# An eight-batch gated scan with a routed expert: statistics, normalising and turning of the next x moved to other engines

## The reference, cut to what matters

```
n = layernorm(x)                                   # over the 256 features
logits = n @ gate_W                                # 4 mixers; the best 2, softmax over them
for m in 0..3:
  g, v, d = n @ Wg[m] + bg[m], n @ Wv[m] + bv[m], n @ Wd[m] + bd[m]
  a = 0.001 + 0.998 * sigmoid(d)
  h[m] = scan over the tokens: h_t = a_t * h_(t-1) + sigmoid(g_t) * tanh(v_t)
t = x + layernorm(sum over m of weight[m] * h[m])
z = layernorm(t) * ln_g + ln_b
e = argmax(softmax(batchnorm(mean of z over the tokens) @ Wr + br)); gate = its probability
y = (relu(z @ W_down[e] + b_down[e]) @ W_up[e] + b_up[e]) * gate
out = t + layernorm(y)
```

## Time and profile before

| | us |
|---|---|
| median of 3 runs | 713.51 |
| profiled execution, whole time | 712.26 |
| its span on the core | 710.5 |
| TensorE busy | 646.5 (91%) |
| VectorE busy | 597.7 (84%) |
| ScalarE busy | 459.0 (65%) |
| GpSimd busy | 123.3 (17%) |

### The profile page before, as it was taken

One profiled execution on the slowest core, in us unless ns is written; L12 is line 12 of the kernel. 1 busy time (PEld: TensorE's weight loads), 2 busy tenths in 40 slices (PEclk: granted clock), 3 DMA queues, 4 the chain that ended last, 5 costly groups with the idle time before them and its releaser, 6 DMA issues. The chain is left out here.

```text
span 710.5 us, 11434 instructions
## 1 busy us (share of the span) xinstructions
PE 646.5 (91%) x3609; PEld 351.4 (49%) x3609; DVE 597.7 (84%) x1320; ACT 459.0 (65%) x813; POOL 123.3 (17%) x182
## 2 busy tenths in 40 slices
PE   3999989999999999999999999999999999898163
PEld 2445545555545555555545555555544554454151
DVE  6584999889997889889997889889997889788946
ACT  2748648875787548775787548775787545866113
POOL 2001032004310052004410052003410032001201
PEclk9999999999999999999999999999999999999555
DMA  8700130020202030020202030020200010000003
GB/s 225 193 1 0 60 119 1 1 71 27 94 1 71 3 123 1 1 71 22 99 1 70 3 123 1 1 71 21 100 1 11 3 60 0 12 1 0 0 12 118
DMA packets 34595, 31.86 MB, mean 45 GB/s; under 512 B 5814, under 2 KB 34522, under 8 KB 34522
## 3 DMA queue, kind: packets, MB, share of 16 engines
q1 hardware_dynamic: 34524, 31.00, 13.9%
HBM read 21.03 MB, written 8.39 MB: 41 GB/s over the span
## 5 line engine op out<-in xcount | busy, mean ns | idle before, releaser
L1192 PE MATMUL ps_main<-xh,w_hi 128*128 128x512 f16 x768 | 292.3, 381 | 2.4 <-ACT xh L512 1.5
L1192 PE MATMUL ps_main<-xh,w_lo 128*128 128x512 f16 x768 | 292.3, 381 | 0.0
L1192 PE MATMUL ps_main<-xl,w_hi 128*128 128x512 f16 x768 | 292.1, 380 | 0.0
L800 DVE TENSOR_TENSOR_SCAN hid<-decay_s,value_s 128x1024 f32<-128x1024 f32 (+1 forms) x64 | 144.6, 2260 | 6.7 <-DVE value_s L820 1.4
L533 ACT ACTIVATE decay_s<-ps_main,vecs 128x512 f32<-128x512 f32 x128 | 88.5, 692 | 61.8 <-PE ps_main L1192 57.4
L533 ACT ACTIVATE value_s<-ps_main,vecs 128x512 f32<-128x512 f32 x128 | 88.8, 694 | 60.4 <-PE ps_main L1192 60.4
L533 ACT ACTIVATE gate_s<-ps_main,vecs 128x512 f32<-128x512 f32 x128 | 88.1, 688 | 54.8 <-PE ps_main L1192 52.8
L1192 PEld LDWEIGHTS ps_main<-xl,w_hi 128*128 128x128 f16 x768 | 75.4, 98 | 91.4 <-issue 1.4
L1192 PEld LDWEIGHTS ps_main<-xh,w_hi 128*128 128x128 f16 x768 | 75.4, 98 | 87.1 <-ACT xh L512 1.8
L1192 PEld LDWEIGHTS ps_main<-xh,w_lo 128*128 128x128 f16 x768 | 75.3, 98 | 83.1 <-issue 0.8
L813 DVE SCALAR_TENSOR_TENSOR mixed<-ps_aux,comb,mixed 128x256 f32<-128x256 f32 x192 | 77.2, 474 | 16.8 <-PE ps_aux L1202 15.0
(11 more groups left out here) (167 smaller groups left out, 636.5 us busy)
## 6 DMA issues: line engine op xcount, KB each, us to landing
x_in<-in_L_attn_x SPq DMA_DIRECT2D x16, 512.0 KB, 4.4
resid<-in_L_attn_x SPq DMA_DIRECT2D x7, 1024.0 KB, 5.2
out<-resid SPq DMA_DIRECT2D x7, 1024.0 KB, 4.5
expert<-experts SPq DMA_DIRECT2D x8, 192.5 KB, 2.2
w_stage<-in_L_attn_Wg SPq DMA_DIRECT2D x4, 256.0 KB, 3.8
w_stage<-in_L_attn_Wd SPq DMA_DIRECT2D x4, 256.0 KB, 5.4
w_stage<-in_L_attn_Wv SPq DMA_DIRECT2D x4, 256.0 KB, 5.5
u_split<-in_L_ffn_W_down SPq DMA_DIRECT2D x4, 256.0 KB
```

The costliest lines, as they stand in the source:

```text
L800: dve.tensor_tensor_scan(states(pc), staged(decay_s, pc, pc.c), staged(value_s, pc, pc.c), start, ALU.mult, ALU.add).then_inc(scanned, 1)
L1192: ins = pe.matmul(ps_main[:, i % BANKS], w[:, 3 * m + kind, k, half * P:(half + 1) * P], v[:, bt.par, k, chunk(c)], start=(n == 0), stop=( ...
```

## The change

- **Statistics of the next x.** VectorE's 8 bn_stats go. ScalarE reads x twice: `sum_x` (8 copies with an accumulated row sum, ahead of banks 1 to 4) and `square_x` (8 squares of x minus mean with an accumulated row sum, ahead of banks 6 to 9). GpSimd makes the mean after the first and scale and shift after the second (`fold_x`, 5 small operations in place of 11).
- **Two copies of the normalised x.** `normalise_x` on ScalarE now writes fp16 directly (`x_tok`, high part, tokens on partitions) and stands ahead of banks 12 to 15. GpSimd makes the same rows in fp32 (`plain_x`, 8 tensor_scalar of 128x256, new), behind `fold_x` and ahead of `power`. VectorE subtracts them in two operations of 128x1024 (`split_x`), where `low_x` stood.
- **Turning by DMA.** `turn_x`, `high_x` and `low_x` are gone for all batches but the first. SyncE issues two transposing DMAs, one for the high and one for the low part, 128x2048 fp16 each, ahead of the expert's load. Products and gates wait for `x_fed`. The next load of x waits for `x_plain` in place of `x_normed`.
- **Positions.** With pv: normalise_t, turn_u, high_u, shares, router, route, down, high_h, turn_h of mixer 1, up and the start of the mix each stand one bank later.
- **Router mean of the last batch.** `sum_rows`, `shift_sum` and `rows_in` are gone; `route_in` sums the accumulators of the four `high_u` copies, as in the other batches, so it stands behind both turn_u.

The diff, cut (the first part is SyncE, then GpSimd, ScalarE, VectorE, TensorE):

```diff
@@ -359,9 +366,19 @@
                 sp.dma_start(resid[:, b.par], x_t[bass.ds(b.n, 1)].rearrange("a p t d -> p (a t) d")
                              ).then_inc(resid_loaded, 16)
 
+            def turn_x(b):
+
+                for half, split in ((0, xh_split), (1, xl_split)):
+                    sp.wait_ge(split, b.n)
+                    if half == 0:
+                        sp.wait_ge(main_filled, EVAC * b.n - EVAC + 1)
+                    sp.sem_inc(turn_begun, 1)
+                    sp.dma_start_transpose(x_feat[:, b.par, half].rearrange("p t k j -> p (t k) j"),
+                                           x_tok[:, half].rearrange("p t d -> p (t d)")).then_inc(x_fed, 16)
...
             def run(j, r, full=True):
                 b, back = Batch(2 * j + r, r % 2, False), Batch(2 * j + r - 1, 1 - r % 2, False)
+                turn_x(Batch(2 * j + r + 1, 1 - r % 2, False))
                 load_expert(back)
...
-                pool.tensor_tensor(mom[:, 1], even[:, :, 2], odd[:, :, 2], ALU.add)
-                link(pool.tensor_tensor(mom[:, 4], mom[:, 3], fold_const["square"][:], ALU.mult))
-                link(pool.tensor_tensor(mom[:, 3], mom[:, 4], mom[:, 1], ALU.add))
-                pool.tensor_tensor(mom[:, 0], even[:, :, 1], odd[:, :, 1], ALU.add)
-                link(pool.tensor_tensor(root_in["x"][:], mom[:, 3], fold_const["eps"][:], ALU.add))
+                pool.wait_ge(x_summed, nx.n)
+                link(pool.tensor_tensor(x_mean[:], x_row_sum[:], fold_const["mean"][:], ALU.mult))
+                pool.sem_inc(x_centred, 1)
+                pool.wait_ge(x_squared, nx.n)
+                link(pool.tensor_tensor(root_in["x"][:], x_row_square[:], fold_const["eps"][:], ALU.add))
                 link(pool.tensor_tensor(root_in["x"][:], root_in["x"][:], neg_half[:], ALU.pow))
-                pool.tensor_tensor(mul_by["x"][:], root_in["x"][:], fold_const["by"][:], ALU.mult)
-                link(pool.tensor_tensor(mom[:, 1], mom[:, 0], neg_half[:], ALU.mult))
-                pool.tensor_tensor(shift["x"][:], mom[:, 1], mul_by["x"][:], ALU.mult).then_inc(x_scaled, C)
+                pool.tensor_tensor(mul_by["x"][:], root_in["x"][:], fold_const["by"][:], ALU.mult).then_inc(x_factor, 1)
+                pool.wait_ge(x_factor, C + nx.n)
+                pool.tensor_tensor(shift["x"][:], x_mean[:], mul_by["x"][:], ALU.mult).then_inc(x_scaled, C)
+
+            def plain_x(nx):
+
+                pool.wait_ge(x_scaled, done(nx))
+                pool.sem_inc(plain_begun, 1)
+                for t in range(T):
+                    ins = pool.tensor_scalar(normed_x[:, t], x_in[:, nx.par, t], mul_by["x"][:, t:t + 1],
+                                             shift["x"][:, t:t + 1], ALU.mult, ALU.add)
+                ins.then_inc(x_plain, 1)
 
             def shift_out(pv):
 
@@ -474,6 +498,7 @@
                 if not pv:
                     bn_power()
                 fold_x(nx)
+                plain_x(nx)
                 if pv:
                     power("a", a_root_in, a_root, pv)
                     power("t", t_root_in, t_root, pv)
...
+                    act.wait_ge(x_loaded[t // (T // C)], 16 * nx.n + 16)
+                    ins = act.activation(normed_x[:, t], x_in[:, nx.par, t], ACT.Copy, accum_out=x_row_sum[:, t:t + 1])
+                if ts[-1] == T - 1:
+                    ins.then_inc(x_summed, 1)
+
+            def square_x(nx, ts):
+
+                act.wait_ge(x_centred, nx.n)
+                for t in ts:
+                    ins = act.activation(normed_x[:, t], x_in[:, nx.par, t], ACT.Square, bias=x_mean[:, t:t + 1],
+                                         accum_out=x_row_square[:, t:t + 1])
+                if ts[-1] == T - 1:
+                    ins.then_inc(x_squared, 1)
+
             def normalise_x(nx, ts):
-                normalise("x", x_in[:, nx.par], x_scaled, x_normed, nx, ts)
+                for t in ts:
+                    act.wait_ge(x_scaled, done(nx))
+                    ins = act.activation(x_tok[:, 0, t], x_in[:, nx.par, t], ACT.Identity, bias=shift["x"][:, t:t + 1],
+                                         scale=mul_by["x"][:, t:t + 1])
+                if ts[-1] == T - 1:
+                    ins.then_inc(xh_split, 1)
 
             def normalise_t(pv, ts):
                 normalise("t", t_rows(pv), t_scaled, u_ready, pv, ts)
...
-                if pv:
-                    NORM_X, HIGH_X, MIX = 7, 12, 28
-                else:
-                    NORM_X, HIGH_X, MIX = 29, 34, 25
+                SUM_X, SQUARE_X, NORM_X, MIX = (1, 6, 12, 29) if pv else (11, 18, 29, 25)
                 for i, bank in enumerate(banks(bt)):
                     if pv:
-                        if 19 <= i < 23:
-                            normalise_t(pv, pair(i, 19))
-                        if i in (23, 24):
-                            high_u(pv, i - 23)
-                        if i == 25:
+                        if 20 <= i < 24:
+                            normalise_t(pv, pair(i, 20))
+                        if i in (24, 25):
+                            high_u(pv, i - 24)
+                        if i == 26:
                             shares(bt)
-                        if i == 27:
+                        if i == 28:
                             router_sigmoids(pv)
-                        if i == 33:
+                        if i == 34:
                             for c in range(C):
                                 hidden_part(pv, c)
-                        if i in (33, 34):
-                            high_h(pv, i - 33)
+                        if i in (34, 35):
+                            high_h(pv, i - 34)
                     elif i == 8:
                         shares(bt)
                     elif i in (3, 9, 15):
                         mixer_high(1 + (i - 3) // 6)
                     if MIX <= i < MIX + 4:
                         start_mix(bt, pv, pair(i, MIX))
+                    if SUM_X <= i < SUM_X + 4:
+                        sum_x(nx, pair(i, SUM_X))
+                    if SQUARE_X <= i < SQUARE_X + 4:
+                        square_x(nx, pair(i, SQUARE_X))
                     if NORM_X <= i < NORM_X + 4:
                         normalise_x(nx, pair(i, NORM_X))
-                    if i in (HIGH_X, HIGH_X + 1):
-                        high_x(nx, i - HIGH_X)
                     evacuate(bt, i, bank, pv is None)
...
+            def split_x(nx):
+
+                dve.wait_ge(x_plain, nx.n)
+                dve.wait_ge(xh_split, nx.n)
+                for c in range(C):
+                    ins = dve.tensor_tensor(x_tok[:, 1, span(c)], normed_x[:, span(c)], x_tok[:, 0, span(c)],
+                                            ALU.subtract)
+                ins.then_inc(xl_split, 1)
...
-                x_moments(nx)
                 scan(pv, pieces(pv)[7])
                 combine(pv, 2)
...
                 scale_t(pv)
-                low_x(nx)
+                split_x(nx)
                 scan(bt, pcs[2])
                 rank_mixers(bt)
                 low_u(pv)
...
                 for c in range(C):
                     scale_t(bt, c)
-                    dve.wait_ge(t_scaled, done(bt, c))
-                    dve.tensor_reduce(shift_sum[:, c:c + 1], shift["t"][:, span(c)], AX.X, ALU.add
-                                      ).then_inc(shift_summed, 1)
                 normalise("t", t_rows(bt), t_scaled, u_late, bt, 1)
-                rows_in(bt)
                 low_u(bt, 0)
+                route_in(bt)
                 route_logits(bt)
                 route_pick(bt)
                 low_u(bt, 1)
...
-                    pe.wait_ge(xl_ready, KT * C * bt.n + KT * (c + 1))
+                if first and pc.plane == 0 and kind == GATE:
+                    pe.wait_ge(xh_ready, KT * (c + 1))
+                    pe.wait_ge(xl_ready, KT * (c + 1))
...
-                        if i == 12:
-                            for c in range(C):
-                                pe.wait_ge(combined, summed_up(pv, 3, c))
-                                turn_x(nx, c)
-                        if i in (22, 24):
-                            c = (i - 22) // 2
-                            low_x_done(nx, c)
+                        if i in (23, 25):
+                            c = (i - 23) // 2
+                            pe.wait_ge(combined, summed_up(pv, 3, c))
                             turn_u(pv, c)
-                        if i == 27:
+                        if i == 28:
                             route(pv)
                             for c in range(C):
                                 low_u_done(pv, c)
                                 turn_h(bt, 0, c)
...
-                sum_rows(bt, 0)
-                pe.wait_ge(combined, summed_up(bt, 3, 0))
-                turn_u(bt, 0)
-                sum_rows(bt, 1)
+                for c in range(C):
+                    pe.wait_ge(combined, summed_up(bt, 3, c))
```

(3 more changed lines are left out.)

142 lines of the change are left out of this document (61 added, 81 removed).

## The result

The changed kernel takes 749.1 us (median of 4 runs, 748.38 to 749.96) against 712.96 us for the kernel before on the same chip: ratio 1.0505, 95% interval 1.0485 to 1.0525. It is 5% slower. The prediction was 752.0 us with a range of 731 to 769, and it was right in sign, size and cause. Several of its terms were not, and they partly cancelled, so it is in part luck that the number came within 3 us.

The account below looks back on a forecast made before the run. TensorE and VectorE's chain to z_wr were taken as equally tight, the chain fed by GpSimd's root_a; 710.5 + 43.8 - 1.8 + 1.0 - 4.4 = 749.1 span, + 1.76 + 1.25 gave 752 us, range 735 to 771 (80%: 731 to 769).

Parts of the forecast that it names:

- The list of GpSimd decides: GpSimd, middle batch: the order fold_x, plain_x, root_a makes VectorE's residual start at T0+28.1 in place of 20.2, +7.9 us.
- (a) The fold held by the scan: GpSimd, middle batch: squares come at T0+18.2, but VectorE's scan holds the fold until T0+20.2; without this, +5.7 us.
- (c) The eight rows: GpSimd, middle batch: plain_x's eight rows between fold and root_a take 3.7 us, to T0+26.4.
- The hole of TensorE: TensorE, middle batch: a hole of about 6 us ahead of turn_u, at T0+35.5 to 42.
- The clock, +0.7 us a batch: TensorE: the hole may drop the granted clock to the lower level, costing 0.7 us a batch, bounds 0 and 2.
- The gain of one bank, 1.3 us: TensorE, middle batch: without x's transposes, 28 banks are done before the route in place of 27, gaining 1.3 us.
- A middle batch, +7.3 us: Each of six middle batches: 7.9 - 1.3 + 0.7 = 7.3 us longer, 43.8 for six.
- First and last batch: Outside the middle batches: first -1.8 us, last batch's main part +1.0 (0 to 1.3), tail -4.4 (bounds -3 and -5).
- Transposing DMAs: SyncE's queue: the two transposes of 512 KB take 4.4 us each and are hidden, with 8 us to spare.
- (b) to (d): GpSimd, after the held fold: fold and power 2.4 us, plain_x's rows 3.7, root_a 1.64, ending at T0+28.1.
- rival of slow transposes: SyncE's queue: transposes of 25 us each make the expert's load 12 us late per batch, 827 us; chance 7%.
- The faster rival: GpSimd: plain_x and root_a do not meet, so only the bank counts in middle batches, 700.5 us; chance 8%.

Follow-up runs that it names:

- e1: The changed kernel with root_a moved ahead of the eight plain_x rows on GpSimd, still behind the fold of the next x: 728.2 us, ratio 1.0209.
- e2: The changed kernel with root_a made on GpSimd before its wait for the squares of the next x: 704.2 us, ratio 0.9878.
- e3: The kernel before plus eight unused GpSimd rows of plain_x's form ahead of root_a, run as soon as x is scaled: 713.31 us, ratio 1.0000.
- e5: The kernel before plus eight unused GpSimd rows ahead of root_a that wait until ScalarE has normalised the next x: 755.8 us, ratio 1.0593.
- e9: The changed kernel with bn_stats on VectorE, the old fold and the normalising ahead of bank 7 as before: 698.78 us, ratio 0.9796.
- e4: The kernel before with only the last batch's router mean taken from the copies, as in the change: 708.54 us, ratio 0.9926.

## Why the prediction was right, step by step

- **The list of GpSimd decides.** Shown by e1 and e2 (21 us, then 24 more, for one position each; in e1 4.5 us less wait gave 3.5, because the rows then run beside residual) and by e3 against e5 (nothing against 42 us for the same eight operations).
- **(a) The fold held by the scan.** Right. The first step stands for 1.45 us and ends at 372.96, and so does the scan, 370.67 + 2.29. The rule of the Trainium skill (SBUF — State Buffer, section Who interferes with whom) agrees with it. e2 shows it the other way round too: VectorE's steps of 0.17 us took 0.39 to 0.53 beside GpSimd's rows.
- **(c) The eight rows.** 4.31 us in place of 3.7. I had taken the output's rows at 0.466 each; these took 0.54. This is the part of the stall that I made too small: root_a ended at T0+28.7 in place of 28.1, and the wait was 8.6 us by the profile where I moved residual by 7.9 (it started at T0+28.9, 8.7 later than before).
- **The hole of TensorE.** Its size was right (5.08 + 0.70, predicted about 6), its place wrong: ahead of bank 21 and not of turn_u. The 2.3 us that I let TensorE lose before it, because ScalarE waits for x_scaled, were 0.93. I had followed only normalise_t, and left out that VectorE, while waiting, also keeps the staging buffers full.
- **The clock, +0.7 us a batch.** The fall came in all six middle batches, for 3 us in two of them and about 7 in four, but cost nothing: all six are 86.7 to 86.9 us long, and the route still waited 0.8 to 0.9 us for z_wr, as before. It was over when turn_u began, and VectorE's chain covered it.
- **The gain of one bank, 1.3 us.** Right for this batch: the route moved from T0+43.5 to T0+52.5, 9.0 us, the period grew by 7.6.
- **A middle batch, +7.3 us.** The argued batch gave +7.6: the route came 9.0 us later, less 1.3 for the bank. My 7.9 for the stall was 0.8 too small and VectorE's chain grew by 0.3, and the 0.7 for a clock that cost nothing stood in for them. That is luck. The six middle batches, from bank 0 to bank 0, grew by 40.6 us or 6.8 in the mean (the lines stand under the next point). The difference to 7.6 is a weakness of method: in the kernel before the batches alternate, 81.1, 79.2, 80.9, 79.2, 80.9 and 79.0 us, and I had read a short one. In the changed kernel all are 86.7 to 86.9. In the first long one TensorE waits 1.47 and 0.40 us for VectorE's `mixed`, a wait that the changed kernel does not have. In the other two the transposes at the batch's start are broken off, with nothing that the profile shows as their releaser:

```profile
412.50 1.74 PE L1202 MATMUL ps_aux<-ident,hid 128*128 128x128 f32 x14
415.49 0.38 PE L1202 MATMUL ps_aux<-ident,hid 128*128 128x128 f32 x2 [1.24 <-issue]
```

The loop's body holds two batches (`run` for r = 1 and 2), and both breaks (1.4 us in all near 253, 1.24 near 415) stand where a new pass of it begins. In the changed kernel the same place shows 0.21 us or nothing. Why is open; TensorE runs 152 matmuls fewer in all (3457 for 3609), but no run tells that apart from its other timing.

- **First and last batch.** TensorE at bank 0 of the second and of the last batch, in the kernel before and then in the changed one:

```profile
91.98 1.91 PE L1202 MATMUL ps_aux<-ident,hid 128*128 128x128 f32 x16
...
572.30 1.91 PE L1202 MATMUL ps_aux<-ident,hid 128*128 128x128 f32 x16
```

```profile
92.00 1.91 PE L1241 MATMUL ps_aux<-ident,hid 128*128 128x128 f32 x16
...
612.91 1.91 PE L1241 MATMUL ps_aux<-ident,hid 128*128 128x128 f32 x16
```

The first batch gains nothing, where I had put -1.8. The 1.75 us of transposes are gone, but TensorE reaches the first transposes of a scan 1.5 us later than before (57.67 against 56.15), and on the way waits 0.66 us for ScalarE's gate_s, ahead of which the new sums stand in ScalarE's list. e2 has the same 0.66 us. e9, which has no such sums, does not: it reaches the transposes at 56.15 and begins its second batch at 90.48. The last batch's main part, up to ScalarE's rows in the tail, takes 99.8 us in place of 99.95, where I had put +1.0: the later route costs nothing there. The tail gains 4.7 (predicted 4.4, e4 alone 4.9).

- **Transposing DMAs.** 4.4 us from issue to landing, as taken, and hidden. By the 350 GB/s of the Trainium skill (Advanced Engine Details and Errata, X-Bar Transpose (TRN2)) it would be 1.5 us, an estimate from that page's rate; the trace shows 4.4, measured from issue to landing. A plain load of 512 KB takes as long here, so the trace agrees with that section's rule that the two are level, and not with the time by its rate.
- **Slips without weight.** All 29 instructions of the window 45 to 48 in the earlier trace rows are matmuls of one column, and not 16. The own terms of (b) to (d) add up to T0+28.0 and not 28.1, and 6 x 12 in the rival of slow transposes is 72 and not 75.

The sum was 38.6 us of span and 35.8 came: +1.8 in the first batch, -3.2 over the six middle ones, -1.15 in the last batch's main part, -0.3 at the end.

The faster rival ("plain_x and root_a do not meet", 700.5 us) failed in the changed kernel for the reason given, since the squares were ready at T0+18.7 (predicted 18.2). Its number is what one gets when they really do not meet: e9, 698.8 us.
